# Perceiver block on one core: keys of the wide cross-attention turned by VectorE and transfers, weight-unit halves moved on VectorE, another order in the causal stage

## The reference, cut to what matters

```
x = x + L0_xattn(layernorm(x), ctx)   # fp8 self-attention and wide cross-attention
x = x + L0_attn(layernorm(x))         # 16 heads, causal softmax attention
x = x + L0_ffn(layernorm(x))          # weights rounded to fp8 in blocks of 32
x = x + L1_xattn(layernorm(x), ctx)   # int8-like cross-attention
x = x + L1_attn(layernorm(x))         # decayed linear attention
x = x + L1_ffn(layernorm(x))          # mixture of experts
```

```
kx, vx = split(ctx @ w_kv_x.T)              # 4096 x 128 each, for a group
kx = layernorm(kx) * kxln_w + kxln_b        # over the 128 of a head
p = softmax(qx @ kx.T * scale)              # 512 query columns x 4096 keys
xout = p @ vx
```

## Time and profile before

| what | value |
|---|---|
| median of 3 runs | 2560.62 us (2558.39 to 2562.17) |
| the profiled execution | 2561.55 us |
| its span | 2559.8 us |
| PE, PEld busy | 89%, 61% of the span |
| DVE, ACT, POOL busy | 70%, 47%, 23% |
| wide stage | about 195 to 1161 us of the span |
| causal stage | about 1226 to 1384 us of the span |

### The profile page before, as it was taken

The page is one execution under the profiler, slowest core; times in us unless marked ns, Lnnn a source line. Parts: engine busy times, 40 slices in busy tenths (PEclk is TensorE's granted clock), DMA queues, the critical chain, the costliest instruction groups (busy, mean ns, idle before and its releaser), DMA issues. The chain is left out here.

```text
span 2559.8 us, 31522 instructions
## 1 busy us (share of the span) xinstructions
PE 2279.4 (89%) x11472; PEld 1556.2 (61%) x11472; DVE 1789.0 (70%) x3422; ACT 1195.6 (47%) x1924; POOL 590.4 (23%) x435
## 2 busy tenths in 40 slices
PE   3779999999999999896897988788888779899998
PEld 2556666666666666464674456555546337677876
DVE  7857887777777778986795976766767763554444
ACT  4443465666665656633332014576666853211111
POOL 7810033333243333350000003323141300000000
PEclk9889999999999999998898999999999989899999
DMA  3331100000010000003454100000000023656661
GB/s 132 115 140 46 47 23 29 9 29 9 29 29 9 30 17 17 4 1 132 173 187 186 56 21 10 1 10 1 6 5 1 21 84 135 218 202 221 230 237 66
DMA packets 47894, 186.93 MB, mean 73 GB/s; under 512 B 6080, under 2 KB 10944, under 8 KB 37504
## 3 DMA queue, kind: packets, MB, share of 16 engines
q1 hardware_dynamic: 47744, 184.95, 19.9%
HBM read 174.97 MB, written 9.96 MB: 72 GB/s over the span
## 5 line engine op out<-in xcount | busy, mean ns | idle before, releaser
L406 PE MATMUL wide_a<-wide_w,ctxT 128*128 128x256 f32 (+1 forms) x2048 | 437.3, 367 | 2.8 <-POOL wide_eps L375 2.8
L406 PEld LDWEIGHTS wide_a<-wide_w,ctxT 128*128 128x128 f32 x2048 | 368.3, 191 | 76.6 <-issue 36.0
L388 POOL TENSOR_TENSOR wide_sums<-wide_sums,wide_s 128x512 f32<-128x512 f32 x224 | 303.9, 1357 | 462.4 <-ACT wide_s L536 449.2
L431 PE MATMUL wide_scores<-wide_q,wide_keysT 128*128 128x512 f32 x512 | 239.0, 605 | 13.9 <-ACT wide_s L532 13.9
L441 PE MATMUL wide_o<-wide_s,wide_values 128*128 128x512 f32 x512 | 233.7, 600 | 3.5 <-ACT wide_s L536 3.5
L532 ACT COPY wide_s<-wide_scores 128x512 f32<-128x512 f32 x256 | 148.7, 586 | 171.2 <-PE wide_scores L431 168.7
L1813 DVE TENSOR_REDUCE int_peaks<-int_a 128x1 f32<-128x1024 f32 x128 | 156.2, 1223 | 92.2 <-PE int_a L1536 91.1
L1536 PE MATMUL int_a<-int_keys,int_qrows 96*128 96x512 bf16 x512 | 150.9, 391 | 58.3 <-DVE int_peaks L1813 32.0
L431 PEld LDWEIGHTS wide_scores<-wide_q,wide_keysT 128*128 128x128 f32 x512 | 87.9, 189 | 150.3 <-ACT wide_s L532 89.4
L1688 ACT ACTIVATE int_prob<-int_a,int_shift,int_qscale 128x1024 uint8<-128x1024 f32 x128 | 155.6, 1217 | 49.5 <-PE int_a L1536 49.3
L594 DVE TENSOR_TENSOR wide_top<-wide_top,wide_s 128x512 f32<-128x512 f32 x240 | 165.9, 691 | 14.0 <-ACT wide_s L532 8.3
(11 more groups left out here) (425 smaller groups left out, 4287.8 us busy)
## 6 DMA issues: line engine op xcount, KB each, us to landing
moe_gate_up<-hbm_m_gu SPq DMA_DIRECT2D x34, 1408.0 KB, 6.1
moe_down<-hbm_m_down_a SPq DMA_DIRECT2D x34, 512.0 KB, 7.0
causal_wqkv<-hbm_wqkv SPq DMA_DIRECT2D x8, 1536.0 KB, 6.5
ctxT<-hbm_ctxT SPq DMA_DIRECT2D x4, 2048.0 KB, 14.8
oproj_raw<-hbm_wproj SPq DMA_DIRECT2D x8, 1024.0 KB, 5.1
ctxT_again<-hbm_ctxT SPq DMA_DIRECT2D x4, 2048.0 KB, 21.4
wide_unit<-hbm_ffn_units SPq DMA_DIRECT2D x28, 256.0 KB, 2.6
ffn_early<-wide_unit SPq DMA_DIRECT2D x28, 256.0 KB, 2.0
```

The costliest lines, as they stand in the source:

```text
L388: ins = pool.tensor_tensor(sums[0][:, :], before, part[:, j, :], ALU.add)
L406: mm = pe.matmul(a[h][:, j, cols], ctxT[:, kc, t * P:(t + 1) * P], w[g % 2][:, kc, cols], start=(kc == 0), stop=(kc == KC - 1))
L431: pe.matmul(sp_[j % 2][:, :], keysT[:, j, :], q[:, :], start=True, stop=True).then_inc(s_s, 1)
```

## The change: what it does

In the wide stage PE no longer turns the keys. VectorE transposes the normalised keys in squares of 32 x 32 (`squares`), one transfer stores them in the chip's memory, four transfers bring them back with the squares in their places (`landed`), and ScalarE scales them into `keysT` (`scale_keys`, now behind `keep(n, 1)`). The PSUM buffer that this frees becomes a third buffer of scores. The queries get two buffers, loaded a group ahead. The unit halves move on VectorE from the end of a pass to the place behind `normalise`. One unit (number 5) moves to the causal stage, and the last slots fall away. In the causal stage the transposes of probabilities come one projection later, and `weigh` of the second head comes behind the scores.

```diff
-FFN_LATE = [6, 22, 7, 23] + [u + n for n in range(8, 16) for u in (0, 16)]
+FFN_LATE = [6, 22, 5, 7, 23] + [u + n for n in range(8, 16) for u in (0, 16)]
...
-    slots += [n for n in range(2 * QPG + 4, N) if n % QPG not in (2, 3) and n != N - 4]
+    slots += [n for n in range(2 * QPG + 4, N) if n % QPG not in (2, 3) and n < N - 6]
...
-        b = st.ps("turned", [P, 4, P])
+        sp_ = [st.ps(f"scores{i}", [P, COLS]) for i in range(3)]
...
+                def send_squares(n):
+                    sp.wait_ge(s_sq, n + 1)
+                    if n >= 2:
+                        sp.wait_ge(s_back[n % 2], 64 * (n // 2))
+                    sp.dma_start(keys_dram[n % 2], squares[:, :, :, :].rearrange("p b t i -> p b (t i)")).then_inc(s_sent, 16)
+
+                def fetch_keys(n):
+                    sp.wait_ge(s_sent, 16 * (n + 1))
+                    if n >= 1:
+                        sp.wait_ge(s_kt, n)
+                    for c in range(4):
+                        sp.dma_start(landed[32 * c:32 * (c + 1), :, :, :].rearrange("p a t i -> p a (t i)"),
+                                     keys_dram[n % 2][:, c, :].rearrange("(a j) x -> j a x", j=32)).then_inc(s_back[n % 2], 16)
...
-                        if i >= 2:
-                            pe.wait_ge(s_se, i - 1)
-                        pe.matmul(sp_[j % 2][:, :], keysT[:, j, :], q[:, :], start=True, stop=True).then_inc(s_s, 1)
+                        if i >= 3:
+                            pe.wait_ge(s_se, i - 2)
+                        pe.matmul(sp_[i % 3][:, :], keysT[:, j, :, :].rearrange("p a i -> p (a i)"), q[g % 2][:, :], start=True, stop=True).then_inc(s_s, 1)
...
-                    if 1 <= n <= N:
-                        turn(n - 1)
...
-                    ins.then_inc(s_kn, 1)
+                    link(ins)
+                    if n >= 1:
+                        dve.wait_ge(s_sent, 16 * n)
+                    dve.transpose(squares[:, :, :, :].rearrange("p b t i -> p t b i"), keys[n % 2][:, :, :].rearrange("p t (b i) -> p t b i", i=32)) \
+                       .then_inc(s_sq, 1)
...
+                    for k in [k for k in range(2 * FFN_EARLY) if slots[k] == n]:
+                        (scale_unit, round_unit)[k % 2](k // 2)
                     if LAG - 1 <= n < N + LAG - 1:
                         shift(n + 1 - LAG)
...
-    due = [(NL * p + 1) // NP for p in range(NP + 1)]
+    due = [NL * p // NP for p in range(NP + 1)]
```

More of the change, by code:

```diff
@@ L305, in wide_cross_attention_stage @@
     slots = [n for n in range(1, QPG) for _ in range(2)] + list(range(QPG, 2 * QPG + 2))
-    slots += [n for n in range(2 * QPG + 4, N) if n % QPG not in (2, 3) and n != N - 4]
+    slots += [n for n in range(2 * QPG + 4, N) if n % QPG not in (2, 3) and n < N - 6]
     slots = slots[:2 * FFN_EARLY]
     with Stage(nc, "wide") as st:
-        q = st.sb("q", [P, COLS])
+        q = [st.sb(f"q{i}", [P, COLS]) for i in range(2)]
         keys = [st.sb(f"keys{i}", [P, 4, D]) for i in range(2)]
-        keysT = st.sb("keysT", [P, 4, P])
+        squares = st.sb("squares", [P, 4, 4, 32])
+        landed = st.sb("landed", [P, 4, 4, 32])
+        keysT = st.sb("keysT", [P, 4, 4, 32])
+        keys_dram = nc.dram_tensor("keys_by_squares", (2, P, 4, P), F32, kind="Internal").ap()
         values = [st.sb(f"values{i}", [P, 4, D]) for i in range(VR)]
@@ L328, in wide_cross_attention_stage @@
         a = [st.ps(f"a{i}", [P, 2, 2 * D]) for i in range(2)]
-        sp_ = [st.ps(f"scores{i}", [P, COLS]) for i in range(2)]
-        b = st.ps("turned", [P, 4, P])
+        sp_ = [st.ps(f"scores{i}", [P, COLS]) for i in range(3)]
         o = [st.ps(f"o{i}", [P, COLS]) for i in range(2)]
         f = st.ps("rows", [P, 4, P])
-        s_ql = st.sem("q_loaded")
+        s_ql = [st.sem(f"q_loaded{i}") for i in range(2)]
+        s_sq, s_sent = st.sem("squares_turned"), st.sem("squares_stored")
+        s_back = [st.sem(f"keysT_loaded{i}") for i in range(2)]
         s_unit = [st.sem(f"unit_loaded{i}") for i in range(2)]
         s_early, s_stored = st.sem("unit_turned"), st.sem("unit_stored")
-        names = ("constants products kept var std normed turned keysT scores s_kept top topT peak rows peak_rows shifted exp summed "
+        names = ("constants products kept var std keysT scores s_kept top topT peak rows peak_rows shifted exp summed "
                  "weighed total half put values values_kept dve pool")
-        (s_c, s_a, s_kv, s_var, s_std, s_kn, s_t, s_kt, s_s, s_se, s_top, s_tt, s_pk, s_row, s_pr, s_sub, s_exp, s_sum,
+        (s_c, s_a, s_kv, s_var, s_std, s_kt, s_s, s_se, s_top, s_tt, s_pk, s_row, s_pr, s_sub, s_exp, s_sum,
          s_o, s_tot, s_half, s_put, s_vp, s_vk, s_dve, s_pool) = (st.sem(n) for n in names.split())
@@ L354, in _ @@
                 load_unit(0)
                 load_unit(1)
-                for n in range(N):
-                    if n % QPG == 0:
-                        g = n // QPG
-                        if g >= 1:
[L360 to L365, removed]
+                for n in range(N + 1):
+                    if n >= 1:
+                        send_squares(n - 1)
+                        fetch_keys(n - 1)
+                    g = n // QPG
+                    if n % QPG == 1 and g + 1 < NG:
+                        if g >= 1:
+                            sp.wait_ge(s_a, 2 * QPG * g)
+                        sp.dma_start(w[(g + 1) % 2][:, :, :], wkv_dram[g + 1]).then_inc(s_w[(g + 1) % 2], 16)
+                    if n % QPG == 2 and 1 <= g and g + 1 < NG:
+                        load_queries(g + 1)
@@ L443, in weigh @@
                     mm.then_inc(s_o, 1)
[L445 to L448, removed]
-                    for j in range(4):
-                        mm = pe.transpose(b[:, j, :], keys[n % 2][:, j, :], C["ident"][:, :])
-                    mm.then_inc(s_t, 1)
                 def turn_top(g):
@@ L665, in _ @@
                         put(g - 1, n % QPG - 2)
-                    for k in [k for k in range(2 * FFN_EARLY) if slots[k] == n]:
-                        (scale_unit, round_unit)[k % 2](k // 2)
                 for piece in range(1, 3):
@@ L897, in _ @@
                         project_out(p - 2, 1)
+                    if p < NP:
+                        project(p, 1)
                     if 1 <= p <= NP:
@@ L900, in _ @@
                     if p < NP:
-                        project(p, 1)
+                        project(p, 2)
                     if 1 <= p <= NP:
                         turn_prob(p - 1, 1)
-                    if p < NP:
-                        project(p, 2)
-                    if 1 <= p <= NP:
                         weigh(p - 1, 0)
-                        weigh(p - 1, 1)
                     if p < NP:
@@ L911, in _ @@
                         score(p, 1)
+                    if 1 <= p <= NP:
+                        weigh(p - 1, 1)
             @block.scalar
```

31 lines of the change are left out of this document (19 added, 12 removed).

## The result

The changed kernel takes 2607.5 us (median of 4 runs, 2599.55 to 2614.56), the kernel before 2559.55 (4 runs beside them, 2558.39 to 2562.17). The ratio is 1.018, 95% interval 1.0163 to 1.0197: 48 us slower. The forecast was 2575 with a range of 2546 to 2594: the direction was right, the size was not. The profiled execution took 2603.89 (span 2602.1), somewhat under its median, so the traces, whose spans are 42.3 apart, account for 42 of the 48.

What follows compares the result with a forecast made beforehand. PE's work alone was taken to bound the wide stage. Terms -24.4 + 17.5 + 0.5 + 7.5 + 2.4 + 4.0 + 4.2 + 2.0 + 0.5 = +14.2 gave a forecast of 2575 us, range 2546 to 2594.

Steps and rivals of the forecast that it cites:

- PE's gain: Wide stage, passes 10 to 55: without the transposes and with a third score buffer, passes of 13.77 us, -24.4 us in all.
- 2.4 for weigh: Wide stage: weigh waits for a late exponential once in a group, 6 x 0.4 = +2.4 us (0 to 6).
- The maxima of a group's last chunk: Wide stage, group ends before passes 17, 25, 33, 41, 49: PE waits 3.5 us each for VectorE's maxima, +17.5 us.
- Rival 1: Wide stage group ends: maxima nearly in time, wait 1 us, clock left alone, time 2555 us; chance 0.27.
- The clock: Wide stage: PE's matmuls run slower behind each of five waits for maxima, 1.5 us each, +7.5 us (bounds 0 and 1.7).
- The start: Wide stage up to pass 9: first scores +4.0, passes 2 to 8 +4.2, before pass 9 +0.5 us.
- The round trip: Wide stage: storing and reloading the keys takes 5.9 us (bounds 4.6 and 9), hidden mid-stage but uncovered in pass 1.
- The end of the stage: Wide stage from pass 56: VectorE's chain sets the pace; +1.6, +4.4, less 3.5 and 0.5: +2.0 us (-5 to +10).
- Rival 2: Wide stage: the keys' store and reload take 9 us or more and bind in a 14 us loop; 2592 us, chance 0.15.
- The causal stage: PE's waits for probabilities (about 7 us) go, but one more unit (5.65) loads VectorE: +0.5 us (-4 to +3).

Runs made afterwards that it cites:

- the control: Kernel before the change, with POOL's wide-stage adds left out except the first of each group: 2544.59 us, ratio 0.9942.

## Why the prediction was wrong, step by step

- **PE's gain** was right: plain steps are 13.8.
- **The failed step is the sum over a group.** For passes 10 to 55 the prediction adds -24.4 for PE, 17.5 for the maxima, 7.5 of clock and 2.4 for weigh, +3.0 in all; they took 26.8 us longer. A group from keys 16 to 48 took 122.6 us on average (490.2 / 4), where 116.6 - 8 x 0.53 + 3.5 + 1.5 + 0.4 = 117.8 was forecast.
   - *The larger half is a term put at nothing without a reason, the put pieces.* No sum was made for the passes with the last piece (20, 28, 36, 44, 52). Of the 4.8 us a group, 2.7 are the put step (16.5 for 13.8) and 0.7 the two steps behind it, where ScalarE's score copies wait for late adds; only the 0.4 forecast for weigh stands against them. The put pieces stood in the kernel before as well, but there was slack behind them; now they meet POOL's adds and the slack is gone. Without the adds these steps take 13.8.
   - *The rest is a term that was mis-sized, "The maxima of a group's last chunk".* The wait came where it was forecast, 4.03 us for 3.5. Up to the shift's end the chain is within 0.5 us of the forecast; the maxima behind it take 3.91 for the "maxima 2.9", since the prediction let only the normalisation meet the adds. Before, the exponential came late by ScalarE's own queue: it began at 527.31, when the maxima were over at 527.06, and its adds another 1.9 later. Now it waits for the shift (84.9 us in 43 waits), follows it at once at 542.87, and its adds begin at 544.86, in the last of the maxima. Without a wait the step takes 14.4 (16.2 less 1.80 in the run without most of the adds), and 14.4 + 5.0 = 19.4 was forecast; it took 20.5 at keys 24 and 32, and 21.4 to 21.5 at keys 40 and 48.
- **The kind of cause was right, and the runs show it.** Taking the adds away gives 58 us, and in the middle 37.5 against nothing in the control. Asking for the maxima later gives 28, putting them where no adds are gives 31, with the last passes as before 50. How much is the slowing of VectorE's instructions, and how much ScalarE's waits for finished adds, stays open: with the adds behind the maxima these were back at 690 ns, and little or nothing was won. Rival 1, that the maxima come nearly in time, has a wait of 1.8 only where there are no adds: in the kernel without them, and at the first group's end, which comes before the first adds.
- **The clock** was right in kind and too small. At keys 24 the projection behind the wait takes 5.29 for 3.62, +1.67 where 1.5 was taken, with a granted clock of 0.68 over it, towards the 1.2 GHz level. At keys 40 the transposes of the maxima are slow too (1.12 for 0.66) and the projection takes 5.86: 2.7 in all, over the prediction's bound of 1.7. The granted clock of the whole window is 0.99, close to the 2.4 GHz level, since the slow stretches are short.
- **The start** cost 11.0 us for 8.7. The round trip was right: the squares start at 207.79, the fetches are issued at 210.58, the scaling starts at 213.91, 6.1 behind the squares. The first scores:

```profile
214.87 5.37 PE L457 MATMUL wide_scores<-wide_q,wide_keysT 128*128 128x512 f32 x8 [3.86 <-ACT wide_keysT L558]
```

 They begin 4.8 later than in the earlier trace rows, not 3.4. But 1.7 of this stands ahead of the change: the stage's first projection ran at a granted clock of 0.68 in this execution and its keys were copied at 200.75, for 199.09 in the one of before, while PE began at 195.3 in both. It differs from one execution to the next (in the run with only the causal order, whose wide stage is that of before, the first copy also came 5.5 us behind PE's start, against 3.8), so the forecast of the first scores was right within 0.3. Passes 3 to 8 take 12.1 (12.3 forecast). The last of the start, from the scores of keys 7 to those of keys 8, takes 14.9 for 13.0, where PE waits 1.81 for maxima; +0.5 was put for it.
- **The end of the stage** was near: from the scores of keys 54 (pass 55) on it took 189.8 us against 185.4, +4.4 where +2.0 was forecast. Passes 56 and 57 cost 7.5 (6.0 forecast), what follows gave 3.1 back (4.0 forecast).
- **Rival 2** fell: 5.3 us of waiting for landed keys from 300 to 1180 us. The fetches of 64 KB each land in 2.0 us.
- **The causal stage** was right in sum: 127.7 us from first mask to last (128.0 before), which is 5.9 won by the order and 5.6 lost by the unit. What the prediction had wrong is that PE's waits go away there:

```profile
PE causal_turned L889 <- ACT causal_masked L967: 7.3, 3, 5.7
```

 The new order takes them from 8.2 to 2.8, and the extra unit on VectorE brings them back to 7.3.
- **What stays open**: the version with the maxima first up to pass 55 needs 99.2 us from the first scores to those of keys 8, where before needs 94.7. Its trace shows PE waiting for the scaled keys seven times there, 10.1 us in all; no run of its own was made for it. And 6 of the 48 us between the medians are not in the profiled executions.

## What to carry to other kernels

When work leaves the engine that sets the pace, make the sum for each kind of pass in the period, those with extra work first, and not for the plain pass: here six of the eight steps of a group gained 2.8 us together and the other two lost 8.4. For each instruction of the engine that delivers late, ask what else starts when its predecessor ends; an instruction that a chain releases at once can fall on it. An instruction that is slowed costs nothing while there is slack behind it, so count the slack that the change takes away. And order deliveries by when they are asked for: the maxima first where the pass is long, the exponential first where it is short.

## What the runs showed of the hardware

A VectorE product or subtraction of two 128x512 tiles that stands among POOL's adds takes up to 1.64 us for 0.69, again and again, so that the four of a unit's half go from 2.5 to 6.3 in the rows of the late unit; POOL itself loses little as far as its spans tell, which are rough (5.62 for 5.30). The Trainium skill ("SBUF — State Buffer", Who interferes with whom) says that a VectorE instruction with two SBUF inputs contends with a GpSimd instruction that reads SBUF. The trace agrees, with the maxima's 866 and 691 ns; the prediction had used this section for the normalisation alone.

The length of a wait does not settle what it costs in clock. In the run with only the units moved back, the projection behind a wait of 2.65 us took 5.31, at a granted clock of 0.67 (541.46, shown above). Behind waits of 2.64 (at 782.58) and 3.12 it took 3.62, at 1.00, the 2.4 GHz level:

```profile
421.25 0.66 PE L476 MATMUL wide_rows<-ident,wide_top 128*128 128x128 f32 x4 [3.12 <-DVEq L616]
421.74 3.62 PE L432 MATMUL wide_a<-wide_w,ctxT 128*128 128x256 f32 x16
```

So a price of 1.5 for each wait, as the prediction took it, is a guess within 0 and 2.7 here.
